# A two-layer graph network on one core: one table for two row products of the scatter stage, and per-quad waits for the message gathers

## The chip, the cores and the metric

One core of one Trainium2 chip runs the whole program. The metric is the device time of that core in microseconds (us). A difference of under about 0.3% of it can't be told from no change.

## The reference

Two graph layers run one after the other on 12,500 nodes with 64 features and 212,500 directed edges that are sorted by their destination; each edge has 16 attributes and one of 8 types.

- Layer 0: `h = relu(layernorm(x))`, one message table per edge type, `m[dst] += (A[type] h)[src]` over all edges, and a GRU step `x = x + GRU(m, h)`.
- Layer 1: `h = relu(layernorm(x))`. Every edge gets a score `w2 · relu(W [h_src, attributes, h_dst])`. A softmax of the scores over the edges of one source weights `h_dst`, the weighted rows are summed per source, and a second GRU step gives the output.

All of it is computed in float32, or in bfloat16 parts that add up to it.

## The kernel before

**The work in stages.** Edges lie in 1664 tiles of 128; nodes lie in 100 windows of 128. A *visit* is one tile with one window. There are 1760 visits, as a tile on the border of two windows is visited twice. Four visits are a group, four groups a body (one turn of a loop). Tables made on the chip (`wwin`, `wslot`, `wtile`, `woff`, `wgot`) give window and tile of each visit.

1. *Set-up* (to about 300 us): layer norm, weights, the message table (stored in HBM by SyncE, SP in the profile), and the visit tables.
2. *Gather stage* (about 300 to 2940 us): the GpSimd engine (POOL) gathers the message rows of one tile per indirect DMA (line 774, 1664 of them, four to a group) into `A_g`, which holds 128 tiles, so 32 groups. TensorE (PE) multiplies a one-hot matrix with the gathered rows (`sums0`, line 1208), VectorE (DVE) makes the one-hots (line 1714) and adds the results to `acc` (line 1662). The first 25 bodies also count source windows on DVE, the next 52 compute the place of every edge in source order (lines 1667, 1674, 1182, 1189), and the rest have neither. Alongside, SP loads edge attributes (line 612) and stores them turned (line 605, six DMAs per body); the last six bodies have no such work.
3. *GRU stage* (about 2940 to 3175 us): layer 0's update and layer 1's norm, slot by slot; POOL splits the source part into bf16 parts, ScalarE (ACT) makes the table `q_tab` and SP stores `h` (line 664).
4. *Scatter stage* (about 3175 to 6060 us, function `rows` on four engines): for each visit PE multiplies a turned one-hot `B_DT` with a window's `q_tab` (144 columns, two matmul instructions in f32, line 1294), adds the attributes' part (line 1295, bf16), and multiplies the same `B_DT` with the window's `h` (64 columns, line 1296). ACT copies one-hots (line 993) and results (line 1000), DVE makes one-hots (1877) and the positions (1888), and POOL scatters the 210-element rows by an indirect DMA per visit (line 802). SP loads the turned attributes of a group (line 655).
5. *Attention stage* (about 6060 to 8150 us) and the second GRU step.

**What sets the order around the change.** POOL's `gather` (lines 764 to 776) waits, ahead of each group b, for three things: that the group four before it has landed (`a_g`), that PE is at most six groups behind (`a_mm`), and that ACT has copied the four columns of indices (`a_idx`, `pick`, line 940) into the small area `A_idx`, which has 16 columns. PE waits at the start of a body until all tiles of that body have landed:

```
if not (first(i) and b < 7):
    pool.wait_ge(a_mm, i * (KEPT // GV) + b - 6)
pool.wait_ge(a_idx, i * (KEPT // GV) + b + 1)
```

In the scatter stage SP loads the attributes of a group into one of four buffers once the scatter of the group four earlier has landed (`b_sc`). DVE waits for the same thing ahead of line 1888, and makes the one-hots of the next group after that. PE turns the one-hots of a group ahead of the products of the group before it.

## Time and profile before

| | |
|---|---|
| median of 3 runs | 8300.23 us (8288.54 to 8313.96) |
| the profiled execution | 8314.69 us |
| its span | 8312.9 us |
| mean granted TensorE clock | 0.672 of full speed |
| PE / DVE / POOL / ACT busy | 65% / 56% / 60% / 24% |

Busy time is per engine and engines overlap, so no share is a bound by itself. Each row of a timeline gives the start, the duration, the engine and line, and in brackets how long the engine had been idle and what released it; "issue" means that the engine's own instruction stream came late and "remote" that the releaser isn't in the profile. Stages have different limits, so each must be read by its own rows.

### The profile page before, as it was taken

To read this page: it belongs to the slowest core of one execution; us is meant where nothing else is said; L and a number is where in the kernel's file an instruction comes from. 1 tells how busy PE (TensorE), PEld (TensorE's weight loads), DVE (VectorE), ACT (ScalarE), POOL (GpSimd) and SP (SyncE) were. 2 spreads that over 40 slices of the span, in tenths; PEclk is the share of its full clock that TensorE was granted. 3 is DMA by queue.
4 is the path that set the end of the run, shared out by engine and by line. 5 is a ranking of instruction groups with operands and counts; after the bars stand their busy time and mean duration, and the time that the engine had idled before them with its cause. 6 is when DMAs were issued, how large, how long until landed. Compare 5 with 4: busy or idle time off the path is not lost.

```text
span 8312.9 us, 183284 instructions
## 1 busy us (share of the span) xinstructions
PE 5362.9 (65%) x33595; PEld 4316.2 (52%) x33596; DVE 4680.8 (56%) x20491; ACT 1991.8 (24%) x5537; POOL 5000.7 (60%) x10349
## 2 busy tenths in 40 slices
PE   5433555555533476676666666666668888888885
PEld 2233333333333355566555556656557777777663
DVE  3566677677633373222222222222269999999997
ACT  3000000000000042222222222222235555555553
POOL 0466666666666535666666666656657777777772
PEclk8655555555555576666666666666678898888999
DMA  6222222222222213222222222222233333333332
GB/s 217 48 50 47 46 45 46 45 46 45 46 49 51 51 58 114 87 87 86 84 83 82 83 82 82 82 81 82 82 116 94 94 94 95 93 94 95 94 94 72
DMA packets 1127950, 649.03 MB, mean 78 GB/s; under 512 B 782017, under 2 KB 1031667, under 8 KB 1126900
## 3 DMA queue, kind: packets, MB, share of 16 engines
q1 hardware_dynamic: 989540, 412.36, 20.4%
q0 software_dynamic: 137728, 233.30, 10.0%
q10 hardware_dynamic: 608, 2.55, 0.1%
q8 instruction: 26, 0.43, 0.0%
q14 instruction: 48, 0.39, 0.0%
HBM read 360.62 MB, written 311.42 MB: 81 GB/s over the span
## 4 chain that ended last, share of the span: by engine, by line
issue 18%; PE 15%; another core or an unknown queue 9%; DVE 7%; POOL 7%; ACT 3%; DVEq 1%; DMA 1%; POOLq 1%; SPq 0%; ACTq 0%
PE banks L1294 6%; PE banks L1296 4%; DVE h L1920 2%; PE banks L1341 2%; DVE h L1925 1%; PE banks L1295 1%; ACT ring L993 1%; DVE ring L1931 1%; ACT ring L1000 1%; PE banks L1282 1%; POOL ring L863 1%; DVE acc L1916 1%; DMA rows_by_src<-ring 1%; POOL ring L847 1%
## 5 line engine op out<-in xcount | busy, mean ns | idle before, releaser
L802 POOL DMA_INDIRECT rows_by_src<-ring x1760 | 1753.8, 996 | 1142.0 <-ACT ring L1000 618.4
L774 POOL DMA_INDIRECT wide<-msg_table,ring x1664 | 1643.6, 988 | 1196.7 <-issue 561.6
L1294 PE MATMUL banks<-wide,ring 128*128 x3520 | 1221.6, 443 | 706.5 <-ACT ring L993 393.0
L1208 PE MATMUL banks<-wide,ring 128*128 x3520 | 860.7, 426 | 570.7 <-DVE acc L1662 191.9
L1294 PEld LDWEIGHTS banks<-wide,ring 128*128 128x128 f32 x3520 | 817.7, 285 | 776.2 <-issue 775.3
L1208 PEld LDWEIGHTS banks<-wide,ring 128*128 128x128 f32 x3520 | 783.9, 328 | 656.4 <-issue 655.7
L1296 PE MATMUL banks<-h,ring 128*128 x3520 | 945.6, 361 | 143.5 <-issue 143.2
L1888 DVE COPY ring<-ring 128x4 f32<-128x4 f32 x440 | 78.8, 179 | 1669.6 <-DMA rows_by_src<-ring 1582.1
L1296 PEld LDWEIGHTS banks<-h,ring 128*128 128x128 f32 x3520 | 822.0, 285 | 243.2 <-issue 125.9
L1662 DVE TENSOR_TENSOR acc<-acc,banks 128x64 f32 x1760 | 389.7, 221 | 836.4 <-issue 315.3
L1000 ACT COPY ring<-banks 128x416 f32<-128x416 f32 x880 | 404.4, 514 | 1741.4 <-remote 1061.7
L1341 PE MATMUL banks<-wide,ring 128*128 x5328 | 715.4, 258 | 0.1
L940 ACT COPY ring<-wide 128x4 int32 (+1 forms) x416 | 80.1, 193 | 2549.2 <-DMA wide<-msg_table,ring 2248.4
L1341 PEld LDWEIGHTS banks<-wide,ring 128*128 128x128 bf16 x5328 | 538.8, 107 | 124.0 <-issue 0.3
L1356 PE MATMUL banks<-ring 128*128 128x65 f32 x3552 | 550.5, 304 | 0.6
L1916 DVE SCALAR_TENSOR_TENSOR acc<-acc,ring,banks 128x65 f32 x1776 | 497.1, 280 | 76.5 <-PE banks L1356 2.2
L1295 PE MATMUL banks<-wpair,ring 128*128 128x144 bf16 x1760 | 515.9, 293 | 16.4 <-issue 16.1
L1182 PE MATMUL banks<-ring,tri_b 128*128 128x400 bf16 x416 | 207.7, 515 | 468.2 <-DVE ring L1667 255.7
L1356 PEld LDWEIGHTS banks<-ring 128*128 128x128 f32 x3552 | 488.6, 213 | 38.6 <-POOL ring L847 0.3
L1877 DVE TENSOR_TENSOR ring<-iota_b,kl_all 128x512 bf16<-128x512 bf16 x440 | 305.1, 693 | 301.1 <-issue 188.1
L1920 DVE SCALAR_TENSOR_TENSOR h<-h,w2bc 128x144 f32<-128x144 f32 x1776 | 457.8, 313 | 0.0
L993 ACT CAST ring<-banks 128x512 f32<-128x512 bf16 x440 | 265.7, 604 | 526.7 <-remote 353.3
(322 smaller groups left out, 10373.6 us busy)
## 6 DMA issues: line engine op xcount, KB each, us to landing
h<-rows_by_src SPq DMA_DIRECT2D x1776, 105.0 KB, 2.0
ring<-attr_turned SPq DMA_DIRECT2D x440, 128.0 KB
attr_turned<-ring SPq DMA_DIRECT2D x416, 96.0 KB
rows_by_src<-ring POOLq DMA_INDIRECT x1760
wide<-msg_table,ring POOLq DMA_INDIRECT x1664
msg_table<-ring SPq DMA_DIRECT2D x100, 256.0 KB, 2.0
ring<-attr_by_dst SPq DMA_DIRECT2D x208, 64.0 KB
attr_turned<-ring SPq DMA_DIRECT2D x208, 64.0 KB
```

Of the source, the lines that this page charges most:

```text
L774: g.indirect_dma_start(out=A_g[:, b * GV + u, :], out_offset=None, in_=table[:, :], in_offset=bass.IndirectOffsetOnAxis(ap=A_idx[:, s, u:u ...
L802: g.indirect_dma_start(out=rows_d[:, :], out_offset=bass.IndirectOffsetOnAxis(ap=B_pos[:, s, u:u + 1], axis=0), in_=B_row[:, s, u, :], in_ ...
L1000: a.copy(B_row[:, t, 2 * half:2 * half + 2, 0:ROW_ONE], two(bank[2 + 2 * (t % 2) + half], ROW_ONE)).then_inc(b_row, 1)
L1208: last = mm(bank[s][:, u * HID:(u + 1) * HID], A_D[:, s, u, :], A_g[:, ds(r[u], 1), :].rearrange("p a k -> p (a k)"), start=True, stop=True)
L1294: mm(b[:, 0:H1], B_DT[:, t, u, :], q_tab[:, w, :].rearrange("p a k -> p (a k)"), start=True, stop=False)
L1295: mm(b[:, 0:H1], B_at[:, t, ds(o[u], 1), :].rearrange("p a k -> p (a k)"), wpair[:, :], start=False, stop=True)
L1296: last = mm(b[:, H1:ROW_ONE], B_DT[:, t, u, :], h[:, w, :].rearrange("p a k -> p (a k)"), start=True, stop=True)
L1341: last = mm(b, C_STb[:, t1, u, :], w[:, k * H1:(k + 1) * H1], start=k == 0, stop=k == PARTS - 1)
L1356: last = mm(bank[6 + t % 2][:, u * (HID + 1):(u + 1) * (HID + 1)], C_S[:, t, u, :], C_W[:, t % 2, u, :], start=True, stop=True)
L1662: v.tensor_tensor(t, t, bank[s][:, u * HID:(u + 1) * HID], ALU.add).then_inc(a_acc, 1)
L1916: return v.scalar_tensor_tensor(k, k, C_cr[:, t6, u:u + 1], bank[6 + t6 % 2][:, u * (HID + 1):(u + 1) * (HID + 1)], ALU.mult, ALU.add)
L1920: v.scalar_tensor_tensor(C_V[:, t1, u, 0:H1], C_V[:, t1, u, 0:H1], 0.0, w2bc[:, :], ALU.max, ALU.mult, accum_out=C_raw[:, t1, u:u + 1]).th ...
```

## The change

It does these things:

- The tensor `h` of its own goes. Layer 0's `h` lies in the upper part of `wide`; layer 1's `h` (now `h2`) and `q_tab` are interleaved in `qh`, 208 elements per window (144 of `q_tab`, then 64 of `h2`). In the scatter stage one product of `B_DT` with the 208 columns takes the place of the two with 144 and 64.
- The copies of source ids and places into `recs1` (ACT, two copies) move from slot 51 of the GRU stage to slot 28, since `h2` now overlaps the memory they read; DVE waits for them from the sixth group of windows on.
- The store of `h` (line 664) reads 64 of every 208 elements.
- POOL waits for PE once per quad (four groups, 16 gathers), for the exact number of visit groups that have read the tiles to be overwritten. DVE and one matmul make a table `wread` with these numbers; POOL loads one by register per quad. The first 32 groups are gathered with no such wait.
- `A_idx` has 128 columns, filled by ACT in quarters of 32: 52 copies take the place of 416.
- SP's load of the turned attributes waits for PE to have read the buffer (`b_hr`), not for the scatter.

The diff, cut to its core:

```
-        h = sb("h", [P, NW, HID])
+        h_flat = wide[:, NW * ROW_ONE:NW * (HID + ROW_ONE)]
+        h = h_flat.rearrange("p (w k) -> p w k", k=HID)
+        qh = wide[:, NW * HID:NW * (HID + ROW_ONE)].rearrange("p (w k) -> p w k", k=ROW_ONE)
+        q_tab, h2 = qh[:, :, 0:H1], qh[:, :, H1:ROW_ONE]
...
-                        sp.wait_ge(b_sc[s], 16 * GV * i)
+                        after(sp, b_hr, s, i - 1)
...
-                    sp.dma_start(h_d[:, :], h[:, :, :].rearrange("p w k -> p (w k)")).then_inc(kept, 16)
+                    sp.dma_start(h_d.rearrange("p (w k) -> p w k", k=HID), h2).then_inc(kept, 16)
...
+                    if s == 0 and not first(i):
+                        read = pool.value_load(wread[0:1, ds((i - 1) * (KEPT // GV) + b + NS - 1, 1)], min_val=1, max_val=VGROUPS)
+                        pool.wait_ge(a_mm, read)
+                        turn(pool, "pool")
                     if not (first(i) and b < NS):
                         pool.wait_ge(a_g[s], 16 * GV * (i * (KEPT // BODY) + b // NS))
-                    if not (first(i) and b < 7):
-                        pool.wait_ge(a_mm, i * (KEPT // GV) + b - 6)
-                    pool.wait_ge(a_idx, i * (KEPT // GV) + b + 1)
+                    if b % (IDX // GV) == 0:
+                        pool.wait_ge(a_idx, i * (KEPT // IDX) + b * GV // IDX + 1)
...
-                for s in range(NS):
+                for q in range(KEPT // IDX):
                     if not first(i):
-                        act.wait_ge(a_g[s], 16 * GV * i)
-                    turn(act, "act")
-                    a.copy(A_idx[:, s, :], idx_all[:, ds(i * BODY + s * GV, GV)]).then_inc(a_idx, 1)
-            loop(act, AT_LOOPS, pick)
+                        for s in range(NS):
+                            act.wait_ge(a_g[s], 16 * GV * ((i - 1) * (KEPT // BODY) + (q + 1) * (IDX // BODY)))
+                        turn(act, "act")
+                    a.copy(A_idx[:, q * IDX:(q + 1) * IDX], idx_all[:, ds(i * KEPT + q * IDX, IDX)]).then_inc(a_idx, 1)
+            loop(act, TILES // KEPT, pick)
...
-                if k == T + 1:
+                if k == G_RECS:
+                    act.wait_ge(g_T, G_RECS - 1)
                     act.wait_ge(r_pos, R_STEP * RANK_LOOPS)
                     a.copy(recs1[:, :, 0], src_T).then_inc(r_c, 1)
                     a.copy(recs1[:, :, 1], place_T).then_inc(r_c, 1)
...
+            pe.wait_ge(s_done, 2)
+            mm(bank[4][0:1, 0:TILE_GROUPS], ones[0:N_KEYS, 0:1], done_w[0:N_KEYS, :], start=True, stop=True).then_inc(s_done, 1)
...
-                        mm(b[:, 0:H1], B_DT[:, t, u, :], q_tab[:, w, :].rearrange("p a k -> p (a k)"), start=True, stop=False)
-                        mm(b[:, 0:H1], B_at[:, t, ds(o[u], 1), :].rearrange("p a k -> p (a k)"), wpair[:, :], start=False, stop=True)
-                        last = mm(b[:, H1:ROW_ONE], B_DT[:, t, u, :], h[:, w, :].rearrange("p a k -> p (a k)"), start=True, stop=True)
+                        mm(b, B_DT[:, t, u, :], qh[:, w, :].rearrange("p a k -> p (a k)"), start=True, stop=False)
+                        last = mm(b[:, 0:H1], B_at[:, t, ds(o[u], 1), :].rearrange("p a k -> p (a k)"), wpair[:, :], start=False, stop=True)
...
+            v.tensor_scalar(tile_end[:, :], iota_v[:, 0:TILE_GROUPS], float(GV), float(GV), ALU.mult, ALU.add).then_inc(s_done, 1)
...
+            ch.link(v.tensor_scalar(done_w[0:K, :], tile_end[0:K, :], small[0:K, 22:23], nt[0:K, :], ALU.subtract, ALU.min))
+            v.tensor_scalar(done_w[0:K, :], done_w[0:K, :], 0.0, None, ALU.max).then_inc(s_done, 1)
...
+            ch.link(v.tensor_scalar(wread, bank[4][0:1, 0:TILE_GROUPS], float(GV - 1), None, ALU.add))
+            v.tensor_scalar(wread, wread, 2, None, ALU.arith_shift_right).then_inc(s_done, 1)
...
+                if g >= 5:
+                    dve.wait_ge(r_c, 2 * REC0)
```

## Rows read from the trace of the kernel before

**Rows 1.** Busy of PE, PEld, DVE, ACT, POOL by stretch; granted clock, DMA share, GB/s.
```profile
300.00:910.00 610.00, 213.12 (x936) 189.61 (x936) 384.85 (x833) 18.75 (x97) 376.61 (x392) 0.50 0.26 46
910.00:2272.00 1362.00, 779.10 (x2850) 481.73 (x2851) 957.24 (x5226) 40.58 (x210) 846.95 (x839) 0.50 0.26 46
2272.00:2872.00 600.00, 217.49 (x960) 193.14 (x957) 200.01 (x651) 18.93 (x98) 388.50 (x402) 0.50 0.28 49
3310.00:5990.00 2680.00, 1765.07 (x9834) 1587.55 (x9835) 714.65 (x4090) 580.50 (x1233) 1630.38 (x1637) 0.64 0.27 83
```

**Rows 2.** Groups by line, from the start to 1000 us: gathers and their products.
```profile
L774 POOL DMA_INDIRECT wide<-msg_table,ring x475 | 459.7, 968 | 502.1 <-ACT ring L940 212.7 <-issue 202.2 <-remote 57.1
L1208 PE MATMUL banks<-wide,ring 128*128 x897 | 220.1, 427 | 290.9 <-DVE ring L1714 138.2 <-issue 114.5 <-DMA wide<-msg_table,ring 38.1
```

**Rows 3.** The same two groups, from the start to 2000 us.
```profile
L774 POOL DMA_INDIRECT wide<-msg_table,ring x1092 | 1083.0, 992 | 878.2 <-issue 395.9 <-ACT ring L940 332.9 <-PE banks L1208 86.6
L1208 PE MATMUL banks<-wide,ring 128*128 x2136 | 521.8, 426 | 290.9 <-DVE ring L1714 138.2 <-issue 114.5 <-DMA wide<-msg_table,ring 38.1
```

**Rows 4.** Line 774 by itself: its count and durations, and who waited for it.
```profile
L774 POOL DMA_INDIRECT wide<-msg_table,ring x1664: 938/944/1467, 230.5 to 2877.5; - x185
...
  PE banks L1182: 139.2, 39
```

**Rows 5.** Timeline of two bodies late in the gather stage.
```profile
2509.21 1.96 PE L1208 MATMUL banks<-wide,ring 128*128 x8 [0.94 <-DVE ring L1714]
2514.05 0.22 DVE L1662 TENSOR_TENSOR acc<-acc,banks 128x64 f32 x1 [5.08 <-remote]
2514.76 0.94 POOL L774 DMA_INDIRECT wide<-msg_table,ring  x1 [3.69 <-remote]
...
2521.09 16.57 SPq L605 DMA_DIRECT2D attr_turned<-ring  x6
...
2529.21 0.22 DVE L1662 TENSOR_TENSOR acc<-acc,banks 128x64 f32 x1 [2.66 <-issue]
...
2537.89 0.22 DVE L1662 TENSOR_TENSOR acc<-acc,banks 128x64 f32 x1 [7.25 <-remote]
```

**Rows 6.** Timeline after the last gather: first product of two bodies in a row.
```profile
2880.95 1.96 PE L1208 MATMUL banks<-wide,ring 128*128 x8 [1.39 <-DVE ring L1714]
...
2891.06 1.33 PE L1208 MATMUL banks<-wide,ring 128*128 x5 [1.10 <-DVE acc L1662]
```

**Rows 7.** The page: packets, MB and share of SP's DMA queue; the scatters' group.
```profile
q1 hardware_dynamic: 989540, 412.36, 20.4%
...
L802 POOL DMA_INDIRECT rows_by_src<-ring x1760 | 1753.8, 996 | 1142.0 <-ACT ring L1000 618.4
```

**Rows 8.** Waits in the scatter stage, 3310 to 5990 us: total us, times, longest.
```profile
POOL rows_by_src L802 <- ACT ring L1000: 563.9, 154, 4.5
```

**Rows 9.** Timeline of the scatter stage at the low and at the high clock.
```profile
4004.40 0.46 PE L1294 MATMUL banks<-wide,ring 128*128 x2
4004.98 0.46 PE L1294 MATMUL banks<-wide,ring 128*128 x2
...
4012.01 0.97 POOL L802 DMA_INDIRECT rows_by_src<-ring  x1 [3.38 <-ACT ring L1000]
4013.02 0.79 PE L1294 MATMUL banks<-wide,ring 128*128 x2
...
4013.61 0.33 PE L1295 MATMUL banks<-wpair,ring 128*128 128x144 bf16 x1
4013.73 0.62 PE L1296 MATMUL banks<-h,ring 128*128 x2
4014.14 0.79 PE L1294 MATMUL banks<-wide,ring 128*128 x2
```

**Rows 10.** Line 655, the attributes' load: who waited for it.
```profile
  PE banks L1294: 79.7, 23
```

**Rows 11.** Groups by line: the first of ACT's two copies into recs1.
```profile
L962 ACT COPY acc<-wide 128x1664 f32<-128x1664 f32 x1 | 1.7, 1682 | 0.0
```

More of the change, by code:

```diff
@@ L64 @@
 KEPT = 128
+IDX = 32
 TILE_GROUPS = TILES // GV
@@ L83 @@
 G_LAG = 2 * G_GROUP + 3
+G_RECS = 28
 G_BANK = (2, 3, 7)
@@ L189, in build @@
         wwin, wtile, wslot, woff = (visits[32 * k:32 * k + 1, :] for k in range(4))
-        wfirst = sb("wfirst", [1, VGROUPS], i32)
+        groups_mem = sb("groups", [64, VGROUPS], i32)
+        wfirst, wread = groups_mem[0:1, :], groups_mem[32:33, 0:TILE_GROUPS]
         wgot = sb("wgot", [1, VTAB // BODY], i32)
@@ L258, in build @@
         swin_T = part(big, COLS // 2, NW * H1).bitcast(bf16)
-        q_tab = big.rearrange("p (w j) -> p w j", j=H1)
         p_tab = wide[:, 0:N_WIN * PW].bitcast(bf16).rearrange("p (w j) -> p w j", j=PARTS * H1)
@@ L277, in build @@
         tile_is = [acc_flat[:, 900 * k:900 * k + 888].bitcast(bf16) for k in (3, 4)]
+        tile_end, done_w = (acc_flat[:, k:k + TILE_GROUPS] for k in (5500, 5500 + TILE_GROUPS))
         b_parts = acc_flat[0:1, 4600:4600 + PARTS * BIAS // 2].bitcast(bf16).rearrange("a (k n) -> a k n", k=PARTS)
@@ L295, in build @@
         A_D = groups(ring, NS, P)
-        A_idx = ring[:, 8640:8640 + NS * GV].rearrange("p (s u) -> p s u", s=NS).bitcast(i32)
+        A_idx = ring[:, 8460:8460 + KEPT].bitcast(i32)
         A_at = part(ring, 2 * P, RING).rearrange("p (j n) -> p j n", j=2)
@@ L332, in build @@
         at[0] = 0
-        C_V = groups(h[:, :, :].rearrange("p w k -> p (w k)"), CS, ROW, NW * HID)
+        rows_mem = wide[:, N_WIN * PW:NW * (HID + ROW_ONE)]
+        C_V = groups(rows_mem, CS, ROW, NW * (HID + ROW_ONE) - N_WIN * PW)
         spare = acc_flat
@@ L397, in build @@
         s_bd, s_bp = sem("s_bd"), sem("s_bp")
-        n_in, s_fold, s_dev = sem("g1_in"), sem("s_fold"), sem("s_dev")
+        n_in, s_fold, s_dev, s_done = sem("g1_in"), sem("s_fold"), sem("s_dev"), sem("s_done")
         a_D, a_mm = sem("a_D"), sem("a_mm")
@@ L775, in gather @@
                             out=A_g[:, b * GV + u, :], out_offset=None, in_=table[:, :],
-                            in_offset=bass.IndirectOffsetOnAxis(ap=A_idx[:, s, u:u + 1], axis=0)).then_inc(a_g[s], 16)
-            loop(pool, TILES // KEPT, gather)
+                            in_offset=bass.IndirectOffsetOnAxis(ap=A_idx[:, b * GV + u:b * GV + u + 1], axis=0)).then_inc(a_g[s], 16)
+            gather(0)
+            pool.wait_ge(s_done, 4)
+            with pool.Fori(1, TILES // KEPT) as i:
+                gather(i)
             for j in range(NW // 2):
@@ L969, in _ @@
                         act.wait_ge(s_var, 2 + g - 1)
-                    a.activation(G_sq[:, g % 2, :, :], h[:, 2 * g * G_GROUP:2 * (g + 1) * G_GROUP, :], ACT.Square).then_inc(s_sq, 1)
+                    a.activation(G_sq[:, g % 2, :, :], h2[:, 2 * g * G_GROUP:2 * (g + 1) * G_GROUP, :], ACT.Square).then_inc(s_sq, 1)
                 j = k - G_LAG
@@ L1260, in _ @@
                     for u in range(2):
-                        last = tr(bank[4][0:HID, u * P:(u + 1) * P], h[:, 2 * j + u, :], ident[:, :])
+                        last = tr(bank[4][0:HID, u * P:(u + 1) * P], h2[:, 2 * j + u, :], ident[:, :])
                     last.then_inc(p_T, 1)
@@ L1633, in _ @@
             v.tensor_tensor(cc[0][0:K, :], bank[4][0:K, 0:1], b_sum[0:K, 3:4], ALU.subtract).then_inc(s_cc, 1)
+            dve.wait_ge(s_iotav, 1)
+            v.tensor_scalar(tile_end[:, :], iota_v[:, 0:TILE_GROUPS], float(GV), float(GV), ALU.mult, ALU.add).then_inc(s_done, 1)
             visit_table(0)
@@ L1639, in _ @@
                 v.tensor_scalar(tile_is[j % 2], tile_rel, float(j), None, ALU.is_equal).then_inc(s_is, 1)
+            dve.wait_ge(s_done, 1)
+            ch.link(v.tensor_scalar(done_w[0:K, :], tile_end[0:K, :], small[0:K, 22:23], nt[0:K, :], ALU.subtract, ALU.min))
+            v.tensor_scalar(done_w[0:K, :], done_w[0:K, :], 0.0, None, ALU.max).then_inc(s_done, 1)
             dve.wait_ge(s_kl, BLOCKS)
@@ L1643, in _ @@
                 ch.link(v.tensor_tensor(kl_all[:, c], bank[q][:, 0:VCHUNK], wbase[:, c], ALU.subtract))
+            dve.wait_ge(s_done, 3)
+            ch.link(v.tensor_scalar(wread, bank[4][0:1, 0:TILE_GROUPS], float(GV - 1), None, ALU.add))
+            v.tensor_scalar(wread, wread, 2, None, ALU.arith_shift_right).then_inc(s_done, 1)
             dve.wait_ge(r_c, REC0)
@@ L1796, in spread @@
                 ch.link(v.tensor_reduce(total, xs[:, w, :], AX.X, ALU.add))
-                v.scalar_tensor_tensor(h[:, w, :], per_row(total, n), -1.0 / HID, xs[:, w, :], ALU.mult, ALU.add).then_inc(s_dev, 1)
+                if g >= 5:
+                    dve.wait_ge(r_c, 2 * REC0)
+                v.scalar_tensor_tensor(h2[:, w, :], per_row(total, n), -1.0 / HID, xs[:, w, :], ALU.mult, ALU.add).then_inc(s_dev, 1)
             def root(k, n_of_slot):
@@ L1860, in _ @@
                     dve.wait_ge(s_std, 2 + 12 * (g + 1))
-                    v.scalar_tensor_tensor(h[:, w, :], h[:, w, :], 0.0, per_row(std, n), ALU.max, ALU.mult).then_inc(s_h, 1)
+                    v.scalar_tensor_tensor(h2[:, w, :], h2[:, w, :], 0.0, per_row(std, n), ALU.max, ALU.mult).then_inc(s_h, 1)
             dve.wait_ge(r_c, 2 * REC0)
```

2 lines of the change are left out of this document (1 added, 1 removed).

## The prediction

> **What bounds the kernel now.** I read the stage table first, then the gathers beside their products, then timelines of both stages.
>
> The change touches two long stages. In the gather stage no engine is full: POOL is busy 377 of 610 us, 847 of 1362 and 389 of 600, DVE 385, 957 and 200, PE less [rows 1]. In the scatter stage POOL is busy 1630 of 2680 us, PE 1765 at a mean clock of 0.64 [rows 1].
>
> *Gather stage.* Does PE wait for the gathers, so that a freer POOL would help? By 1000 us POOL has issued 475 gathers and PE has done 897/2 = 448 visits, so 112 groups; POOL is at group 118.75, which is six ahead with one in work: just what its wait on PE allows [rows 2]. At 2000 us it is 1092 gathers (273 groups) against 267 [rows 3]. So POOL is held by PE. But visits are not tiles: 1664 tiles make 1760 visits, 0.945 per visit. The 448 visits have read some 424 tiles, so 51 gathered tiles lie ready, and at 2000 us 1092 - 1009 = 83. PE needs the 16 of its next body. Time in which a gather came last before PE is at most 139.2 us at line 1182 [rows 4] and 38.1 at line 1208, the latter all in the first 1000 us [rows 2, 3]. It is more a label than a wait: data was there, and DVE's one-hot is needed at the same place.
>
> What costs the time there is something else. The three stretches of 610, 1362 and 600 us hold 25 counting, 52 placing and 25 late bodies, so a body takes 24.4, 26.2 and 24.0 us [rows 1], the last with little DVE work. In a late body POOL starts again at 2514.76 after 3.69 us idle, DVE at 2514.05 after 5.08 us, both released by nothing that the profile shows, though the products they waited for ended at 2511.17. From 2521 us on six DMA issues of SP take 16.57 us, adds of DVE that else follow each other in 0.4 us come 2.9 us apart, and DVE stands 7.25 us before 2537.89 [rows 5]. Once the last gather is out, the same body with the same six stores takes 2891.06 - 2880.95 = 10.1 us [rows 6]. So while POOL gathers, there are stretches in which all instruction streams crawl. They end about when POOL pauses.
>
> *Scatter stage.* A group takes 6.55 us: four scatters at 0.97 + 0.30 us are 5.1, and the rest is pauses: POOL waits for ACT's row copy 563.9 us in 154 pauses of 3.66 us [rows 8], 618.4 us in the whole stage, so 169 pauses [rows 7]. Behind ACT is PE: after a pause it runs at the low level of its clock (1.2 GHz), where a visit takes 1.12 us, 4013.02 to 4014.14; at the high level (2.4 GHz) 0.58 us [rows 9].
>
> **The change, part by part.**
>
> *One product for two.* At the low clock a visit is 0.59 us for line 1294, 0.12 for 1295, 0.41 for 1296 [rows 9]. Line 1295 streams 144 columns in 0.12 us, so the f32 pair streams its 144 in 4 x 0.12 = 0.48 us and has 0.11 for a weight load that isn't covered. With 208 columns it is 4 x 0.173 + 0.11 = 0.80 us, then 0.12 for the attributes. Whether the next visit's load is covered the trace doesn't show in this order; from 0 to 0.10 us. So a visit takes 0.92 to 1.02 us, a gain of 0.10 to 0.20; I take 0.15, 0.6 us per group. It counts where POOL waits: 169 pauses x 0.6 us = 101 us less. Bounds: nothing, if the pauses have another cause, and 618 us, if all go.
>
> The Trainium skill (TensorE: Matmul & The Clock Gate, LDWEIGHTS) gives a weight load as its columns / 1.2 in ns, and lets a load overlap a product only on other rows of the array. By this estimate two f32 loads of 107 ns less are 0.21 us per visit, and 145 us in place of 101. The rows show that a load after the bf16 product is covered, so the sum stays with them.
>
> *Earlier load of the attributes.* It is released by PE rather than by the landed scatter. PE waited for these loads 79.7 us in 23 cases [rows 10]; that goes at most, and some of it lay beside other waits: I take 40 us. SP has nothing else there, so nothing is queued behind the new wait. If cover is gone next, DVE's one-hots are, which still wait for the scatter four groups back.
>
> *The waits of the gathers.* Nothing is gained directly, as 51 to 83 tiles lie ready where 16 are needed; bounds: 0 and 139 + 38 = 177 us. The other side: POOL no longer goes in step with PE. It issues 32 groups, 166 us at 1.3 us per gather, from about 230 us on, over the first four bodies; then it goes in bursts of 16 gathers, 21 us. Late in the stage bursts are like that already. If each of the first four bodies takes 29 us in place of about 24, that is 20 us more; I take 20 in all. The end isn't earlier: gathering ended at visit group 410 before (six behind 416), and the new wait ends at 0.945 v + 28 = 416, v = 410 too. In the counting and placing bodies between them (77 of them) I take no change; the bounds are the rivals.
>
> *Indices.* 416 copies on ACT become 52 and ACT is idle 95% of the stage [rows 1]: 0. POOL gets 96 register loads and waits; queued behind each are 16 gathers, needed two bodies later: 0.
>
> *Small parts.* DVE gets five short operations and PE one product in set-up; about 3 us of it lies on the path. The store of `h` becomes 12,800 pieces of 256 bytes. At the mean of SP's queue, 0.204 x 16 x 8312.9 / 989,540 = 27.4 ns per packet [rows 7], it is 22 us of 16 engines, with four groups (26 us) of loads ahead of it: I take 5 us, bounds 0 and 22. The two copies to `recs1` (1.7 us each [rows 11]) delay ACT by 3.4 us at slot 28 in place of slot 51: 0. Wider strides of `h2` and `q_tab`: 0. The attention stage has the same work.
>
> *Sum.* -101 - 40 + 20 + 3 + 5 = -113 us. From the profiled execution's 8314.7 us this is 8201.7; it stands 14.5 us above the median, so against the median 8187.
>
> **The rivals.**
>
> *A, slower: long bursts make the gather stage crawl.* Place: the 77 counting and placing bodies, whose DVE work leaves no slack. For it: late in the stage, with bursts of 16, a body takes 24 us where 10.1 are needed [rows 5, 6], so 14 us go; in the placing bodies POOL is held in step with PE and they take 26.2 us [rows 1]. If longer bursts cost each of the 77 bodies a quarter of those 14 us, 3.5 us, that is 270 us, less the 141 of the scatter stage, with 20 + 8 as before: +157, near 8455. It decides from (141 - 28) / 77 = 1.5 us per body. Against it: the number of gathers is the same, only shifted by some 22 groups. Chance 0.24.
>
> *B, no difference: the scatter stage's pauses come from the crawl, not from PE.* POOL waits for ACT in its place [rows 7], but ACT may be late because its own stream crawls, as DVE's does in the gather stage [rows 5]. A faster product then moves nothing, and 8300 stays. The Trainium skill (Runtime: NRT & Kernel Launch, Instruction fetch mechanics) says that a taken branch out of the sequencer's window makes it fetch a page before it goes on. If the stalls were these, they would come once per loop turn whatever PE does. That no such stretch follows the last gather [rows 6] speaks against it. Chance 0.14. That the change doesn't do what it says is in here: then PE's columns per visit would be unchanged.
>
> *C, much faster: bursts lengthen in the scatter stage.* With 0.6 us of slack per group, and the loads early, POOL may get through one more group before each pause. Half of the 618 us go: -309 + 28, about 8020. Chance 0.12.
>
> **How the numbers follow.** The forecast, a modest gain, has 0.50, and its own range is 8100 to 8260. Faster by over 0.3% (25 us; less can't be told from no change) is 0.50 + 0.12 = 0.62, within 0.14, slower 0.24. The predicted time is the likeliest case's, 8187. The range reaches into C and up to the middle of A: 7970 to 8430 leaves out about a third of C, a little over half of A and a tail of the forecast, together 0.2.
>
> **What would show it.** Right: line 1296 gone, one f32 pair per visit about 0.8 us at the low clock, a visit 0.92 to 1.02 us; POOL's wait for line 1000 near 450 to 500 us; the wait of PE for attribute loads gone; PE's placing bodies still 26 us. Wrong: placing bodies at 28 us or more with bursts of 16 (A); POOL's wait for line 1000 still over 600 us (B), or under 350 (C). A gather stage shorter by over 50 us would mean that POOL's hold on PE was real after all.

## The result, and where the time went

The changed kernel takes 8763.11 us (median of 4 runs, 8757.65 to 8771.3), the kernel before 8307.09 us (4 runs, 8288.54 to 8320.18), measured beside it. The ratio is 1.0554, with a 95% interval of 1.0533 to 1.0576. The prediction was 8187 us with a range up to 8430, so the time lies outside the range and on the side of rival A.

In the change's own line numbers the gathers are line 784 (774 before), the sums' product 1225 (1208), DVE's adds 1686 (1662), DVE's one-hots 1738 (1714), the joint product 1311 (1294 and 1296), the attributes' product 1312 (1295), ACT's row copy 1015 (1000), the scatters 815 (802), and the one-hots of the visit tables in set-up 1657 on DVE and 1173 on PE (1639 and 1158). I first took the first and last start of three lines of the changed kernel from the trace, each line by itself (of the scatters the register move just ahead of each):

```profile
L784 POOL DMA_INDIRECT wide<-msg_table,ring x1664: 938/944/1597, 232.1 to 3371.3; - x185
L1225 PE MATMUL banks<-wide,ring x3520: 314/421/471, 437.1 to 3447.5; 128*128 x196
L815 POOLq MOVE  x1760: 29/29/29, 3686.7 to 6493.7; - x196
```

The same lines before run from 230.5 to 2877.5, 307.4 to 2946.9 and 3188.6 to 6065.1 us. So the difference of the two spans, 8761.7 - 8312.9 = 448.8 us, divides like this:

| part | before | after | difference |
|---|---|---|---|
| start to the first sums' product | 307.4 | 437.1 | +129.7 |
| first to last sums' product | 2639.5 | 3010.4 | +370.9 |
| last sums' product to first scatter | 241.7 | 239.2 | -2.5 |
| first to last scatter | 2876.5 | 2807.0 | -69.5 |
| last scatter to the end | 2247.8 | 2268.0 | +20.2 |

The gather stage lost 500 us and the scatter stage gave back 70. The next view is the table of stretches of the changed kernel (columns as in [rows 1]): counting, placing and late bodies, and the scatter stage.

```profile
437.00:1104.00 667.00, 220.41 (x967) 196.28 (x967) 385.65 (x852) 2.40 (x11) 354.51 (x368) 0.50 0.23 42
1104.00:2764.00 1660.00, 767.51 (x2809) 474.56 (x2808) 946.56 (x5199) 5.45 (x25) 771.35 (x784) 0.50 0.20 36
2764.00:3382.00 618.00, 219.79 (x988) 199.59 (x988) 206.11 (x675) 1.74 (x8) 369.83 (x384) 0.50 0.27 48
3750.00:6430.00 2680.00, 1482.35 (x6699) 1107.59 (x6698) 734.67 (x4200) 578.33 (x1258) 1685.22 (x1677) 0.69 0.29 88
```

The work is the same, and so is TensorE's granted clock: DVE's 5199 instructions take 946.56 us against 957.24 for 5226 before, at 0.50 [rows 1]. Only the stretch around them is longer (1660 us against 1362). The 52 placing bodies take 31.9 us each (25.9 before, counted from the first weight load of one body to that of the next), the 25 counting bodies 26.7 (24.7), the late ones 23.8 (23.5). That makes 52 x 6.0 + 25 x 2.0 = 362 of the 371 us.

What fills the longer body? POOL's gathers in one placing body run unbroken from 1722.46 to 1742.23 us, 16 of them, and the next comes at 1752.98. Three stretches of that body, same columns:

```profile
1722.40:1730.40 8.00, 5.48 (x20) 3.63 (x21) 7.28 (x44) 0.00 (x0) 6.35 (x6) 0.50 0.28 37
1730.40:1744.40 14.00, 3.05 (x12) 1.54 (x11) 4.64 (x21) 0.00 (x0) 9.79 (x10) 0.50 0.22 45
1744.40:1754.00 9.60, 6.55 (x27) 4.00 (x26) 7.38 (x40) 0.22 (x1) 1.02 (x1) 0.50 0.12 27
```

In the first 8 us of the burst DVE does 44 instructions, in the next 14 only 21, and once POOL has paused it does 40 in 9.6 us. PE goes the same way (20, 12 and 27 matmuls), at a granted clock of 0.50 throughout. In the timeline of the middle stretch single instructions of DVE come over 1 us apart:

```profile
1730.32 0.22 DVE L1686 TENSOR_TENSOR acc<-acc,banks 128x64 f32 x1
1732.88 0.22 DVE L1686 TENSOR_TENSOR acc<-acc,banks 128x64 f32 x1 [2.34 <-remote]
1734.27 0.22 DVE L1686 TENSOR_TENSOR acc<-acc,banks 128x64 f32 x1 [1.17 <-issue]
...
1738.59 0.18 DVE L1735 COPY ring<-wide 128x32 bf16 x1 [2.58 <-issue]
```

This is the crawl of [rows 5], now in bodies that did not have it to this degree. The page's groups fit this. The largest part of the idle time before DVE's adds ends with "remote" (314.0 of 898.3 us), and of POOL's before the gathers with "issue" (1026.8 of 1715.2 us; 561.6 before). Of the latter some 0.3 us per gather is the usual distance of two gathers:

```profile
L784 POOL DMA_INDIRECT wide<-msg_table,ring x1664 | 1618.6, 973 | 1715.2 <-issue 1026.8
L815 POOL DMA_INDIRECT rows_by_src<-ring x1760 | 1768.7, 1005 | 1053.9 <-ACT ring L1015 557.8
L1311 PE MATMUL banks<-wide,ring 128*128 x3520 | 1359.6, 516 | 884.4 <-ACT ring L1008 646.0
...
L1686 DVE TENSOR_TENSOR acc<-acc,banks 128x64 f32 x1760 | 389.5, 221 | 898.3 <-remote 314.0
```

To see it over all placing bodies, I laid their bursts over each other. A burst is a run of gathers with starts less than 2.6 us apart. The table is the share of time in which DVE has a data instruction, by the time since the burst's first gather (slices that lie wholly within the burst), and since the end of its last one:

| us since the start | 0-2 | 4-6 | 6-8 | 8-10 | 10-12 | 12-14 | 14-16 | 16-18 | end 0-2 | end 4-6 |
|---|---|---|---|---|---|---|---|---|---|---|
| before, all bursts | 0.87 | 0.84 | 0.90 | 0.41 | 0.43 | 0.80 | 0.61 | 0.46 | 0.53 | - |
| before, the 13 of 16 gathers | 0.89 | 0.83 | 0.94 | 0.55 | 0.45 | 0.85 | 0.65 | 0.46 | - | - |
| after | 0.90 | 0.74 | 0.77 | 0.44 | 0.29 | 0.21 | 0.11 | 0.20 | 0.16 | 0.89 |

(Before, most bursts are over by then: of 89, only 13 last 18 us. After, all 49 last 18 us.) Before, the placing bodies have bursts of 4, 8 and 12 gathers and 13 of 16, in which a quarter of the gathers lie; after, 45 of 16 and few others. The first 8 us of a burst do little harm in either kernel. What follows does: after, DVE falls to a half and then to about a tenth of its pace until POOL pauses. But the time since the start doesn't tell all. Before, the share comes back to 0.80 at 12 to 14 us while the burst goes on, also in its 13 long bursts. Why a burst of 16 does less harm there stays open. What can be said is that bodies are long in the kernels in which nearly all bursts are that long.

The 130 us ahead of the stage have the same form. These are DVE's and PE's lines of the visit tables between 230 and 440 us, grouped by line:

```profile
L784 POOL DMA_INDIRECT wide<-msg_table,ring x128 | 123.0, 961 | 232.4 <-ACT ring L954 193.7 <-issue 35.4 <-DMA wide<-msg_table,ring 3.3
L1173 PE MATMUL banks<-acc 128*128 128x444 bf16 x104 | 33.0, 492 | 146.0 <-issue 78.5 <-DVE acc L1657 67.4
L1657 DVE TENSOR_SCALAR acc<-acc 128x1776 bf16<-128x1776 bf16 x13 | 8.6, 675 | 144.9 <-remote 136.9 <-PE banks L1173 4.1 <-issue 2.7
```

DVE's 13 operations are idle 144.9 us between them; in the kernel before 11.7 us. While POOL issued its first 32 groups without a break, the table that PE needs for its first sums was not finished.

### The profile page after: what moved, and what is told of

Read it like the earlier page. It is cut to its first block, busy times and chain, and to the rows that moved or that the text cites. A ratio compares the mean times of both kernels' runs of the same rounds, so it can differ in the third digit from the quotient of the medians.

```text
span 8761.7 us, 173278 instructions
## 1 busy us (share of the span) xinstructions
PE 5050.2 (58%) x30077; PEld 3813.7 (44%) x30078; DVE 4689.0 (54%) x20496; ACT 1906.4 (22%) x5173; POOL 4983.7 (57%) x10350
## 4 chain that ended last, share of the span: by engine, by line
another core or an unknown queue 18%; issue 14%; POOL 7%; PE 6%; DVE 6%; ACT 4%; POOLq 1%; DVEq 1%; ACTq 0%; DMA 0%; SPq 0%
PE banks L1311 2%; ACT ring L1008 2%; PE banks L1357 2%; ACT ring L1015 2%; DVE wide L1946 1%; DVE wide L1951 1%; POOL ring L860 1%; POOL ring L876 1%; DVE ring L1957 1%; PE banks L1372 1%; POOL ring L857 1%; POOL ring L855 1%; POOL ring L868 1%; POOL ring L849 1%
## 5 line engine op out<-in xcount | busy, mean ns | idle before, releaser
L784 POOL DMA_INDIRECT wide<-msg_table,ring x1664 | 1618.6, 973 | 1715.2 <-issue 1026.8
L815 POOL DMA_INDIRECT rows_by_src<-ring x1760 | 1768.7, 1005 | 1053.9 <-ACT ring L1015 557.8
L1311 PE MATMUL banks<-wide,ring 128*128 x3520 | 1359.6, 516 | 884.4 <-ACT ring L1008 646.0
L1311 PEld LDWEIGHTS banks<-wide,ring 128*128 128x128 f32 x3520 | 798.5, 280 | 1145.2 <-issue 1105.7
L1225 PE MATMUL banks<-wide,ring 128*128 x3520 | 859.7, 426 | 713.4 <-DVE ring L1738 341.5
L1225 PEld LDWEIGHTS banks<-wide,ring 128*128 128x128 f32 x3520 | 784.5, 328 | 797.3 <-issue 796.4
L1686 DVE TENSOR_TENSOR acc<-acc,banks 128x64 f32 x1760 | 389.5, 221 | 898.3 <-remote 314.0
L1357 PE MATMUL banks<-wide,ring 128*128 x5328 | 718.5, 266 | 0.0
L1372 PE MATMUL banks<-ring 128*128 128x65 f32 x3552 | 572.3, 312 | 0.6
L1372 PEld LDWEIGHTS banks<-ring 128*128 128x128 f32 x3552 | 509.2, 221 | 40.1 <-POOL ring L860 0.3
L1946 DVE SCALAR_TENSOR_TENSOR wide<-wide,w2bc 128x144 f32<-128x144 f32 x1776 | 456.1, 311 | 0.0
L1698 DVE SCALAR_TENSOR_TENSOR ring<-ring,banks 128x100 f32<-128x100 bf16 x1664 | 321.7, 254 | 245.6 <-issue 108.0
L1299 PE MATMUL banks<-ident_b,ring 128*128 128x128 bf16 x1760 | 222.7, 265 | 365.9 <-DVE ring L1903 277.6
L1206 PE MATMUL banks<-ring,rest_b 128*128 128x400 bf16 x416 | 190.4, 535 | 367.6 <-remote 185.5
```

The costliest lines, as they stand in the source:

```text
L784: g.indirect_dma_start(out=A_g[:, b * GV + u, :], out_offset=None, in_=table[:, :], in_offset=bass.IndirectOffsetOnAxis(ap=A_idx[:, b * GV ...
L815: g.indirect_dma_start(out=rows_d[:, :], out_offset=bass.IndirectOffsetOnAxis(ap=B_pos[:, s, u:u + 1], axis=0), in_=B_row[:, s, u, :], in_ ...
L1225: last = mm(bank[s][:, u * HID:(u + 1) * HID], A_D[:, s, u, :], A_g[:, ds(r[u], 1), :].rearrange("p a k -> p (a k)"), start=True, stop=True)
L1311: mm(b, B_DT[:, t, u, :], qh[:, w, :].rearrange("p a k -> p (a k)"), start=True, stop=False)
L1357: last = mm(b, C_STb[:, t1, u, :], w[:, k * H1:(k + 1) * H1], start=k == 0, stop=k == PARTS - 1)
L1372: last = mm(bank[6 + t % 2][:, u * (HID + 1):(u + 1) * (HID + 1)], C_S[:, t, u, :], C_W[:, t % 2, u, :], start=True, stop=True)
```

## The experiments

Theory 1 is that the length of POOL's unbroken bursts is the cost: an exact wait that frees whole quads lets POOL issue 16 gathers (128 at the start) in a row, and past some 8 us the other engines' instruction streams crawl. Against it stood that the index area or the joint table's layout costs the time (2, 3), that the set-up's new steps do (4), or that exactness and the longer lead do (5). Chips differ: the kernel before took 8235.48 us on the chip of the first four experiments below (joint table, gather part, inexact wait, held burst) and 8232.62 on that of the last, and 8301.74 to 8310.14 on that of the others. So what is compared across chips is the ratio to the kernel before on the same chip. Times of stages that stand beside each other from different chips can differ by the 0.9% of the chips alone.

**The joint table alone.** Gather part undone:

```
-        A_idx = ring[:, 8460:8460 + KEPT].bitcast(i32)
+        A_idx = ring[:, 8640:8640 + NS * GV].rearrange("p (s u) -> p s u", s=NS).bitcast(i32)
...
-            gather(0)
-            pool.wait_ge(s_done, 4)
-            with pool.Fori(1, TILES // KEPT) as i:
-                gather(i)
+            loop(pool, TILES // KEPT, gather)
```

> The change without its gather part: the waits, the index area of 16 columns and the set-up are those of the kernel before; the joint table and the wait on b_hr stay. Theory 1 (the loss lies in the gather stage alone, and the scatter stage kept its gain of 72 us, 2881 to 2809): 8307 - 72 = 8235, within 8200 to 8265; scatter stage near 2810; first sums on PE at 307, counting bodies 24.7 and placing bodies 25.9 us as before. Theory 2 (part of the loss of the placing bodies comes from the joint table's new places in memory): placing bodies at 28 us or more, time above 8330.

Measured: 8153.92 us against 8235.48, ratio 0.9899 (0.9872 to 0.9926). First sums at 301.4 us, counting bodies 24.5, placing 25.8, scatters from 3160.3 to 5907.8, 2747 us. All of the loss is in the gather part; theory 2 falls.

**The gather part alone**, added to the kernel before, with nothing of the joint table.

> The kernel before with the gather part of the change alone (exact waits by fours of groups, index area of 128 columns, their set-up). Theory 1: the gather stage as in the changed kernel (first sums at 437, counting bodies 26.7, placing bodies 31.9 us), scatter stage 2881 as before: 8307 + 130 + 50 + 311 = 8800, within 8770 to 8850. Theory 2: placing bodies below 30 us, time below 8700.

Measured: 8702.04 us, ratio 1.0566 (1.0540 to 1.0592). First sums at 432.2 us, bodies 26.4 and 31.2: the loss of the changed kernel, in full. The two parts don't simply add up: 1.0566 less the 0.0101 that the joint table gains alone would be 1.0465, and the changed kernel has 1.0554. So beside the long bursts little is left of the joint table's gain; where it goes was not looked for.

**The inexact wait again, all else as changed.**

```
-if s == 0 and not first(i):
-    read = pool.value_load(wread[0:1, ds((i - 1) * (KEPT // GV) + b + NS - 1, 1)], min_val=1, max_val=VGROUPS)
-    pool.wait_ge(a_mm, read)
-    turn(pool, "pool")
+if not (first(i) and b < 7):
+    pool.wait_ge(a_mm, i * (KEPT // GV) + b - 6)
```

> The changed kernel with one thing undone: POOL waits again, before each group, for PE to be at most six groups behind its own number less 32 (the inexact wait of the kernel before); the index area of 128 columns, the table's set-up and the joint table stay. Theory 1 (the freed waits let POOL issue 16 gathers unbroken and the sequencers crawl): bursts mostly of 12 again, placing bodies 26 us, first sums at 307 to 315, time near that of the joint table alone, 8200 to 8270. Theory 3 (the index area, its copies of 32 columns or its one wait per quarter make the bodies long, not POOL's bursts): placing bodies stay at 31 to 32 us, time 8600 to 8760.

Measured: 8165.60 us, ratio 0.9917 (0.9892 to 0.9941). Its counting and placing bodies, in the table of stretches:

```profile
301.00:907.00 606.00, 220.72 (x967) 196.26 (x967) 386.66 (x852) 2.83 (x13) 388.28 (x400) 0.50 0.25 48
907.00:2235.00 1328.00, 765.48 (x2808) 474.31 (x2807) 960.86 (x5198) 5.66 (x26) 840.92 (x829) 0.50 0.24 46
```

The same 5198 instructions of DVE now fit in 1328 us instead of 1660. One wait carries the whole loss. The index area and its few copies cost nothing and gain nothing, as the prediction said; theory 3 falls.

**The first burst held back.** `pool.wait_ge(s_done, 4)` stands ahead of `gather(0)` instead of behind it.

> The changed kernel with POOL's wait for s_done moved from behind its first 32 groups to before them, so that no gather is issued until DVE and PE have built kl_all and the table of waits; all else as changed. Theory 1 (the unbroken first 32 groups slow the set-up of the visit tables by 130 us): the set-up takes as long as before the first gathers, so first sums at 320 to 350 and the time 60 to 120 us less than 8763: 8640 to 8700. Theory 4 (the 130 us are the new steps of the set-up themselves, whatever POOL does): first sums at 437 or later, time 8760 to 8830.

Measured: 8681.74 us, ratio 1.0537 (1.0510 to 1.0563). The ratio is only 0.0017, some 14 us, under that of the changed kernel (8681.74 us is in theory 1's range only because this chip is faster), so both theories missed. The set-up ran freely, as theory 1 said, and the first sums' product came at 312.7 us, earlier than even that theory had it:

```profile
L1173 PE MATMUL banks<-acc 128*128 128x444 bf16 x104 | 21.7, 373 | 23.6 <-DVE acc L1657 23.6
L1657 DVE TENSOR_SCALAR acc<-acc 128x1776 bf16<-128x1776 bf16 x13 | 8.0, 622 | 12.2 <-PE banks L1173 12.1 <-DVE wgot L1584 0.2
```

But nothing was gained by it, because the 25 counting bodies took 32.0 us instead of 26.7, 133 us more. This is their stretch:

```profile
313.00:1113.00 800.00, 220.15 (x967) 195.93 (x966) 382.52 (x847) 3.26 (x15) 458.70 (x478) 0.50 0.20 40
```

The unbroken run of gathers, 144 in this trace from 289.4 to 469.5 us and 126 of them after the first sums' product, now lies over the first bodies and slows them. A burst costs wherever it is put; moving it is not enough, it has to be broken up.

**The exact wait for each group of four tiles** instead of one for four groups (`if not first(i)`, and `b` in place of `b + NS - 1`).

> The changed kernel with the exact wait taken for each group of four tiles instead of once for four groups; the index area in quarters and the joint table stay. Theory 1: PE releases a group every 5 to 6 us, so POOL is held in pieces of 4 to 12 gathers once it has its lead, bodies of the placing part at 25 to 28 us, but the first 32 groups are still unbroken, so first sums at 437: ratio to the kernel before 1.00 to 1.02. Theory 5 (it is the exactness and the longer lead that cost, not the step of four groups): placing bodies above 30 us, ratio 1.04 or more.

Measured: 8302.49 us (10 runs), ratio 1.0003 (0.9990 to 1.0016). Placing bodies 25.5 us, bursts of 4 to 12 again, first sums at 430.9. As exact as the change, and the placing bodies are healed: what hurt them was the step of 16 tiles, not the exactness. Of its 98 bursts 3 have more than 13 gathers. The first burst's 130 us stay. First to last sums' product takes 2980.9 - 430.9 = 2550 us, against 2946.7 - 302.3 = 2644 in a kernel with the inexact wait on the same chip (the joint table with the old load, below): the stage is 94 us shorter with the exact wait, and the first burst takes more than that back. (The two kernels also differ in the index area and in how many tiles lie ready when the stage begins, so the 94 us aren't the wait's alone.)

**A pause of POOL by force.** Exact waits by quads stay; before every second group POOL waits for the group before to land, so a burst has 8 gathers:

```
+if b % 2 == 0 and not (first(i) and b == 0):
+    pool.wait_ge(a_g[(b - 1) % NS], 16 * GV * (i * (KEPT // BODY) + (b - 1) // NS + 1))
```

> The changed kernel with a pause of POOL forced in the gather stage: before every second group POOL waits until the group just before has landed, so no burst has more than 8 gathers; exact waits, index area and joint table stay. Theory 1 (the length of POOL's unbroken bursts is what costs, not how exact its waits are): 8 gathers of 1.25 us and a landing of 2.1 us make 12.1 us, 24.2 us per body of 16, and DVE's bodies no longer crawl (about 22 us), so POOL sets the pace: gathers end near 230 + 104 x 24.2 = 2750, first sums near 305, the time 8763 - 8307 gone and about 100 us more: ratio to the kernel before 0.975 to 0.995. Theory 5 (the exact waits cost by when they release, whatever the burst): placing bodies stay above 28 us, ratio above 1.02.

Measured: 8162.13 us against 8301.74, ratio 0.9837 (0.9812 to 0.9863). Adding waits to the changed kernel makes it 7% faster. Its three kinds of body:

```profile
301.00:849.00 548.00, 216.41 (x969) 196.28 (x969) 382.86 (x855) 2.40 (x11) 342.00 (x356) 0.50 0.28 50
849.00:2176.00 1327.00, 768.24 (x2807) 474.97 (x2806) 949.63 (x5197) 5.66 (x26) 845.29 (x847) 0.50 0.25 46
2176.00:2705.00 529.00, 217.40 (x990) 200.28 (x991) 205.98 (x683) 2.18 (x10) 330.20 (x338) 0.50 0.30 54
```

Counting bodies take 21.9 us, placing 25.5, late 20.3; first sums at 300.6. The last bodies take 21.8 us where they took 9.4, since PE now waits there for POOL's own pace. Placing bodies were expected at 22: a burst of 8 lasts 10 us, and DVE's share is still down to 0.57 in its last two. The last gather starts at 2822.5 us where 2750 was expected. Theory 5 falls.

**The same pause in the scatter stage too** (`pool.wait_ge(b_sc[1], 16 * GV * (i + 1))` ahead of group 2, `b_sc[3]` ahead of group 0).

> The same with a pause in the scatter stage too: before every second group of scatters POOL waits for the landing of the group just before. Theory 1: bursts of 8 scatters, 8 x 1.28 + about 2.1 = 12.3 us, 220 of them 2710 us, against 2750 to 2810 of the scatter stage in the changed kernel, and little crawl: 40 to 100 us less than the run beside it without this pause. Theory 6 (a scatter lands later than a gather, or PE and ACT are the bound of this stage with or without the crawl): the pauses add, the stage is 2800 us or longer and the time higher than the run beside it.

Measured: 8128.04 us, ratio 0.9797 (0.9771 to 0.9823), 34 us below the run beside it. The scatters take 2766 us (2796 in the run beside it), between the two expectations: 8 scatters and the landing take 12.4 to 12.6 us, as said, and the stage is then POOL's. This timeline is of POOL in that stage:

```profile
4508.26 0.97 POOL L821 DMA_INDIRECT rows_by_src<-ring  x1 [0.30 <-issue]
4511.51 0.97 POOL L821 DMA_INDIRECT rows_by_src<-ring  x1 [2.27 <-DMA rows_by_src<-ring]
...
4523.93 0.97 POOL L821 DMA_INDIRECT rows_by_src<-ring  x1 [2.39 <-DMA rows_by_src<-ring]
```

**Both pauses with the inexact wait.**

> The changed kernel with both pauses (gathers and scatters in bursts of at most 8) and with the inexact wait of the kernel before in place of the exact one. Theory 1 (with short bursts it hardly matters which of the two waits POOL has, since POOL's own pace of 24.2 us per body is the bound): within 20 us of the run with both pauses and exact waits, which stood at 0.980 of the kernel before. Theory 7 (once the bursts are short the longer lead of the exact waits pays, since PE is never held by the placing part's slower bodies): 40 to 100 us slower than that, 0.985 to 0.992.

Measured: 8175.89 us, ratio 0.9844 (0.9827 to 0.9862). The exact waits are worth some 0.0047 x 8300 = 39 us once bursts are short: the counting bodies take 23.3 us here and 21.9 with them. The intervals just fail to overlap (0.9823 and 0.9827), so the gain is barely clear of noise; theory 7's lower end is nearer than theory 1.

**The kernel before with nothing but the two pauses.**

> The kernel before with nothing but the two pauses (POOL waits for the landing of the group before at every second group, in the gather and in the scatter stage). Theory 1: its gather stage crawls 590 us of 2570 and its scatter stage 474 of 2881, bursts of at most 8 take most of it away: first sums at 307, bodies of 22 to 25 us, 60 to 150 us less, ratio 0.982 to 0.993. Theory 5 (the crawl is not set by the length of bursts): the pauses only add, ratio 1.00 or more.

Measured: 8140.12 us against 8310.14, ratio 0.9804 (0.9786 to 0.9821), better than theory 1 said. Two waits of POOL make a kernel as fast as the best one here, with no joint table and no exact waits. Of the 170 us 134 lie in the scatter stage; the placing bodies, at 25.5 us, are hardly shorter than the 25.9 before. POOL's waits in its scatter stage, 3250 to 5800 us, are no longer for ACT (563.9 us in [rows 8]):

```profile
POOL rows_by_src L808 <- DMA rows_by_src<-ring: 261.9, 110, 2.6
POOL rows_by_src L808 <- ACT ring L1006: 0.9, 3, 0.3
```

Its scatters take 5880.2 - 3137.7 = 2742 us, less than the 2765 and 2766 of the two kernels with the joint table and both pauses. So with short bursts the product that the change saves is hidden behind POOL.

**The joint table with the old wait of the attribute loads** (`sp.wait_ge(b_sc[s], 16 * GV * i)`).

> The kernel with the joint table alone, its attribute loads waiting again for the scatter's landing instead of for PE. Measures the term of the earlier load by itself: the prediction put it at 40 us, so this would be slower by 40 than the joint table with the early load (0.990 of the kernel before): 0.995. Against it: the load is hidden either way, 0.990, and the joint product alone carries the gain of the scatter stage.

Measured: 8228.08 us, ratio 0.9904 (0.9886 to 0.9921), against 0.9899 with the early load: no difference that can be told. By the view of [rows 10], who waited for the line of the loads, this kernel has

```profile
  PE banks L1302: 128.8, 76
```

against 79.7 us in 23 cases before, 3.7 with the joint table and the early load, and 2.6 in the changed kernel. So the faster product made PE wait for these loads more often, the early load took that away, and its removal moved nothing. The list of all waits puts fewer down to these loads as the last releaser, 3.9 us before and 37.9 here.

**What makes the others crawl: SP's traffic, or POOL alone?** SP's attribute loads and stores cut to one partition, in the same number of transfers; the attribute part of the output isn't computed.

> The changed kernel with SP's attribute traffic of the gather stage cut to one partition of 128 (both the loads and the stores of every body); the turned attributes are filled once with other values before, so the attribute part of the output is not computed, and the stage begins late by that fill. Only its placing bodies are read. Theory 1a (a long burst of POOL alone is enough to make the other queues crawl): placing bodies stay at 30 to 32 us. Theory 1b (the crawl needs SP's stores falling into a burst): placing bodies at 22 to 26 us although POOL still issues 16 gathers unbroken.

Measured in one execution (9103.82 us; the first body alone takes 217 us, since the loads wait for the fill): placing bodies 33.3 us, bursts of 16. This is their stretch:

```profile
1342.00:3072.00 1730.00, 768.74 (x2806) 473.19 (x2805) 941.49 (x5191) 5.44 (x25) 765.01 (x784) 0.50 0.08 15
```

The DMA engines are busy 8% instead of 20% and move 15 GB/s instead of 36, and the bodies are no shorter. It isn't SP's load on the DMA engines; theory 1b falls. That SP issues nothing at all was not tried. This holds although the prediction's timeline of [rows 5] had SP's long issue right beside the stall.

**Does any gap do?** The pause placed after the first gather of the next group, so that one transfer stays in flight:

```
 for u in range(GV):
+    if u == 1 and b % 2 == 0 and not (first(i) and b == 0):
+        pool.wait_ge(a_g[(b - 1) % NS], 16 * GV * (i * (KEPT // BODY) + (b - 1) // NS + 1))
+        turn(pool, "pool")
```

> The kernel with both pauses, exact waits and joint table, but each pause starts one transfer later: POOL waits for the landing of the group before only after it has issued the first gather (or scatter) of the next group, so that one transfer is always in flight and the pause is about 1.25 us shorter. Theory 8 (any gap in POOL's issue keeps the queues from crawling): POOL's pace becomes about 11.2 us for 8, 22.5 us per body, little crawl: scatter stage 2500 to 2650 instead of 2771, time 100 to 250 us below the run with the full pauses (0.980), so 0.950 to 0.968. Theory 9 (the queue has to drain, so a gap that leaves a transfer in flight counts as the same burst): crawl of 300 us or more comes back in the scatter stage, placing bodies above 27 us, ratio 0.985 or higher.

Measured: 8528.41 us against 8232.62, ratio 1.0359 (1.0337 to 1.0381). POOL's gap is there, but the burst isn't broken by it. These are its gathers in a placing body:

```profile
1507.69 0.95 POOL L787 DMA_INDIRECT wide<-msg_table,ring  x1 [0.30 <-issue]
1509.69 0.94 POOL L787 DMA_INDIRECT wide<-msg_table,ring  x1 [1.05 <-issue]
...
1517.70 0.95 POOL L787 DMA_INDIRECT wide<-msg_table,ring  x1 [0.30 <-issue]
1525.43 1.38 POOL L787 DMA_INDIRECT wide<-msg_table,ring  x1 [6.78 <-PE banks L1234]
```

Placing bodies take 29.8 us (31.2 in the gather part alone, on a chip as fast) and the first sums come at 422.4. A gap of 1.05 us with a gather in flight helps little, one of 2.3 us with an empty queue keeps the bodies at 25.5. So theory 9 holds in the gather stage (bodies over 27 us, ratio over 0.985). The scatter stage bears out neither theory: the scatters take 2752 us, about as long as with the full pauses (2766 on a slower chip) or with the joint table alone (2747), so no crawl of 300 us came back there and nothing was gained. The loss of this run lies in the gather stage and ahead of it. Whether it is the empty queue or the length of the gap isn't told apart, since this edit changed both.

## Why the prediction was wrong, point by point

- **The freed waits gain nothing directly** (bounds 0 and 177): mis-sized. The stage was up to 94 us shorter with exact waits for each group, and the whole 39 with pauses. It is small beside what follows. The upper bound was also read short: the 38.1 us at line 1208 are up to 2000 us, and the whole trace has 56.6.
- **"In the counting and placing bodies I take no change"**: this is the step that failed. They took 2.0 and 6.0 us more each, 362 us. The prediction had seen the crawl, that it comes only while POOL gathers, and that late bodies with bursts of 16 pay 14 us. It then put weight on the argument that the number of gathers is the same, only shifted. The number isn't the cost: with the same 1664 gathers in runs of at most 8 the placing bodies take 25.5 us. The length of the runs is. POOL's wait for PE, in step with it, had cut the gathers into runs: three quarters of them lay in runs of at most 12, and in the changed kernel only 1 in 100 did.
- **The first 32 groups, +20 us over four bodies**: mis-sized. They cost 130 us, and in the set-up, not in the bodies: the burst starts at 232 us, and PE's first sums wait for a table that was built in that time. The prediction put the burst on PE's bodies without asking what was still on the path when it began.
- **Rival A** (chance 0.24) was the case. Its place was right, its price of 3.5 us per body was not: the 77 bodies paid 4.7 us on average, and the set-up 130 on top where it had 20.
- **The joint product**: the mechanism was right. At the low clock a visit takes 0.91 us (predicted 0.92 to 1.02, before 1.12), as two products after each other show:

```profile
4000.66 0.99 PE L1311 MATMUL banks<-wide,ring 128*128 x2
...
4001.57 0.99 PE L1311 MATMUL banks<-wide,ring 128*128 x2
```

  That is 0.21 us less per visit. The Trainium skill (TensorE: Matmul & The Clock Gate, LDWEIGHTS) led to an estimate of 0.21 against the 0.15 that I took from the rows: the trace agrees with the page at this level of the clock. At the high level (granted clock 1.00) it doesn't. A visit takes 0.46 us there, 0.58 before, so 0.12 us less:

```profile
4004.67 0.56 PE L1311 MATMUL banks<-wide,ring 128*128 x2
...
4005.13 0.56 PE L1311 MATMUL banks<-wide,ring 128*128 x2
```

  The stage as a whole gained 69.5 us here, 88 with the joint product and the old load (scatters 3186.3 to 5974.5, on a chip where the kernel before took 8310), where 101 were predicted for the product. The size is near, the way there was another. POOL's pauses of over 1 us went from 179 of 3.28 us to 150 of 3.37: fewer, as in rival C, and not shorter by 0.6 us each (both beyond the usual distance of 0.3 us). The bursts became 12 (130 of them, before 91 of 12 and 57 of 8), and its wait for ACT is 557.8 us, not 450 to 500.
- **Rival B** (0.14) was partly right, and stronger than I gave it: with the bursts cut, the old product loses nothing (ratio 0.9804 against 0.9797; against 0.9844 for the joint table with the same inexact wait and the same pauses, it is even ahead by 36 us, 28 of them after the last scatter). That the pauses which the joint product shortens come in good part from the crawl is argued from this and from the 134 us that POOL's pauses alone take off the stage; it isn't shown directly. The Trainium skill (Runtime: NRT & Kernel Launch, Instruction fetch mechanics) was cited for it as the possible cause. The profile's page of the changed kernel shows that the two instruction queues carried 25 and 48 packets in the whole execution:

```profile
q8 instruction: 25, 0.41, 0.0%
q14 instruction: 48, 0.39, 0.0%
```

  The crawl comes in nearly every one of 100 bodies, so fetches over these queues, as far as the profile shows them, aren't it. What it is stays open.
- **Earlier attribute loads, -40**: mis-sized. The wait went (79.7 to 2.6 us), the time did not (0.9904 and 0.9899 with the late and the early load). In the list of waits by their last releaser these loads held PE for only 3.9 us before; the prediction took its term from the view that counts 79.7.
- **Indices 0, set-up +3, `recs1` 0**: right as far as the runs show: with the inexact wait again, all of it stays in, and the time is that of the joint table alone within the intervals (0.9917 and 0.9899). The store of `h`, +5: the time from the last sums to the first scatter is 2.5 us less. Not foreseen: 20 us more after the last scatter. On the chip of the middle experiments the kernels with the joint table, the change's set-up and its index area take 2263 to 2265 us from the last scatter's own row to the end, those without 2235 and 2245. The run with both pauses and the inexact wait has it too, so it isn't the exact wait. Nor is it the set-up and index area by themselves, for the gather part alone takes 2242 us (the kernel before as well), or the joint table by itself (2245 and 2247): it comes with both together. Its cause was not looked for.

## What to carry to other kernels

Before loosening a wait, ask what else it does: a wait that holds only an engine with time to spare (POOL waited for PE 126.0 us in all before) can still be what spaces out a stream of indirect DMAs. Look at the run lengths of POOL's issues beside the progress of the other engines, and where these slow down try to break the runs by waiting for your own last transfer (every 8 here, the only length that was tried); here two such waits, in the old kernel, are worth 2% by themselves. And when a burst has a cost, moving it (as the held start did) only moves the cost.

## What the runs showed of the hardware

- While POOL issues indirect DMAs without a break, PE and DVE can run through their instructions slowly after the first 8 us or so (placing bodies of the changed kernel). DVE's share of time with a data instruction falls from 0.90 to between 0.11 and 0.44 while TensorE's granted clock stays at 0.50, and is back at 0.89 within 4 to 6 us of the last gather. In the kernel before, bursts as long did less harm (0.45 to 0.85); what makes the difference isn't known.
- The load that SP's transfers put on the DMA engines isn't the cause: without most of it the engines' busy share was 0.08 in place of 0.20, and the bodies stayed long (33.3 us).
- With a pause of 2.3 us until the last transfer has landed, after every 8 gathers, the placing bodies take 25.5 us; with a gap of 1.05 us and one transfer in flight they take 29.8.
- POOL itself hardly notices: a gather's median is 944 ns in the kernel before, in the changed one and in those with pauses. So its own row never shows the harm that it does.
- Two f32 weight loads less per visit, at the same number of columns, are 0.21 us at the low level of TensorE's clock (1.12 to 0.91) and 0.12 us at the high level (0.58 to 0.46).
